# One named table load per normalising stage on ScalarE, in a kernel of a state-space block, attention and routed experts

## The reference

```python
# layer 0: normalise over 256 channels, split in 4 branches, scan each in 4 directions
xn = _ln(x, ln_g, ln_b)                      # xc * rsqrt(var + eps) * g + b
x = silu(conv3x3(xi @ in_W) + conv_b)        # each branch
delta = softplus(dts @ dt_W + dt_b)
h = h * exp(delta * A) + (delta * u) * B     # 2304 steps, 16 states; y = h . C
y = _ln(sum of the 4 directions, og, ob) @ out_W + skip_scale * xi
y = _ln(concatenate(outs), ln_g, ln_b) @ proj_W + proj_b
# layer 1: attention over all 4608 tokens, then 2 of 8 experts for each token
t = _ln_t(tokens)
f = t / max(norm(t), 1e-12)
a = softmax(f @ f.T) @ f
t1 = tokens + l2norm(0.8 * f + 0.2 * a)
out = t1 + sum over top 2 experts of p_e * (gelu(_ln_t(t1) @ W1_e + b1_e) @ W2_e + b2_e)
```

## Time and profile before

| | |
|---|---|
| runs of before | 6272.69, 6276.89, 6279.28 us (median 6276.89) |
| span of the profiled execution, first to last instruction | 6270.2 us |
| busy PE, DVE, ACT, POOL | 82%, 68%, 62%, 67% of the span |
| both norms, merge, project, blend | 0 to 98 us (with setup), 4085 to 4450, 4450 to 4613, 5536 to 5695 |
| scan | 780 to 4085 us |
| attention | 4613 to 5536 us |

### The profile page before, as it was taken

One profiled execution on the slowest core, in us unless ns is written; L12 is line 12 of the kernel. 1 busy time (PEld: TensorE's weight loads), 2 busy tenths in 40 slices (PEclk: granted clock), 3 DMA queues, 4 the chain that ended last, 5 costly groups with the idle time before them and its releaser, 6 DMA issues. The chain is left out here.

```text
span 6270.2 us, 83748 instructions
## 1 busy us (share of the span) xinstructions
PE 5167.0 (82%) x21564; PEld 3423.2 (55%) x21564; DVE 4275.8 (68%) x4244; ACT 3892.7 (62%) x8375; POOL 4196.6 (67%) x2703
## 2 busy tenths in 40 slices
PE   4666389999898898998989999845589999965997
PEld 2333155555555555555555555522358888844776
DVE  2666589999999999999999999956231111143433
ACT  2655488888888888888888888834532222233233
POOL 0566589999999999998999999933014444412343
PEclk8888599999999999999999999977789999975898
DMA  3454477777777777777777777764200000013213
GB/s 94 148 186 181 183 241 250 248 248 247 243 250 239 249 247 244 248 247 238 247 246 247 251 246 249 243 216 164 91 18 0 0 0 0 0 38 107 70 58 128
DMA packets 399686, 1073.56 MB, mean 171 GB/s; under 512 B 51470, under 2 KB 94511, under 8 KB 393600
## 3 DMA queue, kind: packets, MB, share of 16 engines
q1 hardware_dynamic: 384544, 1038.35, 49.7%
q0 software_dynamic: 7584, 20.72, 1.0%
q10 hardware_dynamic: 7104, 9.44, 0.5%
HBM read 883.39 MB, written 184.94 MB: 170 GB/s over the span
## 5 line engine op out<-in xcount | busy, mean ns | idle before, releaser
L918 POOL TENSOR_TENSOR scan_hc<-scan_h,scan_c_rep 128x768 f32<-128x768 f32 x1536 | 2749.4, 1824 | 236.7 <-PE scan_ps_y L749 171.4
L749 PE MATMUL scan_ps_y<-scan_hc,keep_ident 128*128 128x512 f32 (+1 forms) x6144 | 2217.2, 489 | 23.5 <-ACT scan_y L784 23.1
L883 DVE TENSOR_TENSOR_SCAN scan_h<-scan_da,scan_h,scan_ps_p 128x768 f32<-128x768 f32 x896 | 1567.8, 1794 | 0.0
L749 PEld LDWEIGHTS scan_ps_y<-scan_hc,keep_ident 128*128 128x128 f32 x6144 | 1066.6, 190 | 822.5 <-issue 737.6
L801 ACT ACTIVATE scan_warm<-scan_du_t 128x128 f32<-128x128 f32 x4608 | 1423.7, 388 | 40.7 <-PE scan_ps_p L740 35.3
L840 ACT ACTIVATE scan_da<-scan_dd,layer_a_neg 128x768 f32<-128x768 f32 x1344 | 1184.2, 921 | 2.2 <-issue 1.6
L1260 POOL TENSOR_TENSOR attn_e_lo<-attn_e,attn_e_hi 128x512 fp32r<-128x512 f32 x324 | 417.6, 1289 | 771.4 <-DVE attn_e_hi L1251 771.4
L740 PE MATMUL scan_ps_p<-keep_ident,scan_warm 128*128 128x128 f32 x4608 | 645.9, 277 | 221.9 <-DVE scan_h L883 221.1
L883 DVE TENSOR_TENSOR_SCAN scan_h<-scan_da,scan_ps_p 128x768 f32<-128x768 f32 x448 | 758.4, 1734 | 2.1 <-ACT scan_da L840 2.0
L740 PEld LDWEIGHTS scan_ps_p<-keep_ident,scan_warm 128*128 128x128 f32 x4608 | 531.5, 142 | 371.8 <-issue 160.4
L862 DVE TENSOR_TENSOR scan_ps_p<-scan_ps_p,scan_dd 128x768 f32<-128x768 f32 x576 | 546.6, 949 | 185.9 <-PE scan_ps_p L732 185.0
(11 more groups left out here) (291 smaller groups left out, 7109.4 us busy)
## 6 DMA issues: line engine op xcount, KB each, us to landing
scan_c_rep<-bc_dram SPq DMA_DIRECT2D x1536, 384.0 KB, 4.1
scan_dd<-dd_dram SPq DMA_DIRECT2D x96, 768.0 KB, 5.6
scan_b_rep<-bc_dram SPq DMA_DIRECT2D x192, 384.0 KB, 4.7
dd_dram<-delta_de SPq DMA_DIRECT2D x96, 384.0 KB, 6.5
dd_dram<-delta_du SPq DMA_DIRECT2D x96, 384.0 KB, 15.7
y_dram<-scan_y SPq DMA_DIRECT2D x96, 384.0 KB, 4.5
merge_y<-y_dram SPq DMA_DIRECT2D x32, 1152.0 KB, 10.3
delta_img<-xn_dram SPq DMA_DIRECT2D x16, 576.0 KB, 10.1
```

The source lines that it names most:

```text
L749: mm = pe.matmul(ps_y[:, lo:hi], keep["ident"][:, :], hc[t % HR][:, lo:hi], start=n == 0, stop=n == N - 1)
L883: dve.tensor_tensor_scan(view(h[n]), view(x), view(y), start, ALU.mult, ALU.add).then_inc(scan_done, 1)
L918: pool.tensor_tensor(hc[t % HR][:, :], h[t % N][:, :], c_rep[t % CR][:, :], ALU.mult).then_inc(hc_done, 1)
```

## The change

At the head of ScalarE's stream in four stage functions (five calls, as `norm_phase` is called twice) one call is added that loads a table set by name; the set holds Ln and Exp together.

```diff
@@ -46,6 +46,7 @@
 ROUND = 12582912.0
+LOG_EXP = "natural_log_exp_and_others"
@@ -253,6 +254,7 @@            (norm_phase)
         @block.scalar
         def _(act):
+            act.preload_act_table_set(LOG_EXP)
             with act.Fori(0, NTT // LN) as i:
```

## The result

The changed kernel takes 6235.96 us (median of 4 runs, 6227.41 to 6241.17) against 6277.69 for the kernel before on the same chip: ratio 0.9931, 95% interval 0.9912 to 0.9951. That is 42 us less, where 55 were forecast (6222 us, 6205 to 6237). A second measurement, on another chip, gave 6220.43 us (5 runs) against 6277.35: 0.9913, 0.9899 to 0.9927, which is 57 us less. The two intervals overlap; between them lies 0.992, about 50 us.

What follows compares the result with a forecast made beforehand. No engine is busy all the time; chains in the normalising stages make ScalarE's loads count where exposed. Loads 48.9, clashes 2.5 and clock 4 sum to 55.4 us, taken as 55: 6276.9 - 55 = 6222 us, range 6205 to 6237.

Steps and rivals of the forecast that it cites:

- The Exp's loads: All normalising stages: the table load ahead of each of 28 Exps is exposed, 1.43 us each, 40.0 us saved.
- the clock: TensorE in merge and project: shorter idle times may keep its granted clock from falling; 4 us gained, between -4 and 12.
- the clashes: Merge: VectorE and GpSimd taking turns on a shared port; shifted meeting dates bring +2.5 us net, between -8 and +12.
- The Ln's loads: Loads ahead of Ln, mostly hidden under TensorE's sums: 7.2 us saved in merge, 1.7 in project and blend, 0 in norms.
- The added loads: Five named loads ahead of ScalarE's first wait of each stage: hidden, cost 0; up to 5.1 us if four were uncovered.
- The page's 2.66 us a switch: Rival: every table load also stalls ScalarE for a drain, 2.66 us in all, giving 6186 us; chance 2%.
- the signs it named: In merge, if right: VectorE's L1019 mostly under 6 us, and L1003 longer than 2.88 us in most rounds.
- The norms: The two norm stages, four rounds: only the load ahead of Exp is exposed, 4 x 1.43 = 5.7 us saved.
- The total: Whole kernel: 48.9 + 2.5 + 4 = 55.4 us saved, forecast as 55, giving 6222 us.
- its own range: Whole kernel: 6209 to 6234 us, held at 71%, said to follow from the bounds of its uncertain terms.
- Merge gives its part back: Rival: GpSimd's turn in merge, bound to its input's landing, becomes the limit; 18.6 + 2.5 us missing, 6243 us; chance 10%.
- The built program has the same ones elsewhere: Setup, delta, scan and experts: no new table load appears there, as the built program keeps the same loads.

## Why the prediction was right, and which terms were mis-sized

- **The Exp's loads, 40.0 us:** the mechanism was right. 0.43 to 0.48 us from the last Ln's start to the first Exp in every round, and 44 us by the medians or 35 by the stages when they are put back. The sum taken alike in all stages was not: each is worth 1.8 us in project and blend, where the clock adds to it, and in merge, put back alone, nearly nothing, because of the clashes.
- **The Ln's loads, 8.9 us:** right. VectorE's wait in merge fell by 2.33 us, the sum of 0.90 and 1.43, and the Ln's loads put back cost 10.5 us by the medians and 5 by the stages, far from the 36 of full price.
- **The added loads, 0:** right, and three of the five are not needed at all.
- **The page's 2.66 us a switch:** by the rows 1.28 us; the Exp behind a put-back load starts 0.01 us after it. The Trainium skill (ScalarE: Activation LUTs, What ACT_TABLE_LOAD costs) has a drain in its sum that no run here shows as time of its own.
- **The clock, taken at 4 us, "nearer to 0, because both idle times are still long":** mis-sized. It is worth 1.1 us a round in merge (measured without the clash), some 9 us in eight rounds, and what project and blend gave over their loads, 15.7 + 14.9 - 24.6 = 6 us, is the same sign and is put down to it too (L1127 from 7.13 to 5.83 us). 15 us in place of 4. That the clock is what makes these steps long was tested by filling the idle time.
- **The clashes, taken at +2.5, between -8 and +12:** mis-sized, with the wrong sign. Without GpSimd's sum merge gains 26.8 us, with it 16.2: the clash takes back some 10 us. Merge scatters by 7 us between executions, so whether that is beyond the bound of -8 isn't certain. The prediction counted the two clashes as independent costs of each round. They are coupled: a late L1003 delays L1019 into GpSimd's next work, so both fall into one round and the next is free. Of the signs it named, L1019 is over 10 us in three rounds, as often as it was over 9 before, and L1003 is longer than 2.88 us in four rounds of eight, not in most.
- **The norms, 5.7 us:** 3.4 were found in the stage lengths. VectorE's wait for the Exp in norm1 fell from 9.23 to 7.81 us in each round, which is the forecast 1.42. TensorE's first step of a round there lies between 9.4 and 11.1 us in the traces of before and of the change, so norm1's rest of 1 us is within that scatter; norm0's of 1.5 us stays open.
- **The total:** the normalising stages give 50.2 us, and 42 and 57 us in the two measurements lie on both sides; delta and scan scatter by more than that difference. That 55 came so near is in part luck: the clock gave 11 us more than its term and the clashes took 13 more, and the two errors cancel. The first measurement, 6235.96 us, lies 1 us inside the range of 6205 to 6237, and outside what the prediction calls its own range, 6209 to 6234. That upper end doesn't follow from its terms either: clashes of -8 and a clock of -4 would give 6222 + 10.5 + 8 = 6240.
- **The rivals:** none came in. The nearest, "Merge gives its part back", had the mechanism (GpSimd's turn, bound to the landing of its input, becomes the limit), at some 10 us in place of its 21.
- **"The built program has the same ones elsewhere":** true, but I drew no rival from it. That a named load outlives its stage was to be seen in the built programs, and no rival had it.

## What to carry to other kernels

Price a removed instruction by its place, not by its length: between two steps of the same engine it shortens the chain by its length and a bit more, under the pace of the engine that feeds it by nothing. Whether the stage gets shorter by as much is a second question, and here merge and project answered it differently. When a chain gets shorter against a partner that keeps its own clock (here GpSimd, bound to a transfer), write down for two rounds in a row where they meet; one round alone misses the alternation. And before a table set is named in every stage, look how far one naming reaches.

## What the runs showed of the hardware

- The group of six VectorE steps with both inputs in SBUF (L1019 in the kernel before, L1021 in the changed one) takes 2.9 us alone and 10.6 us where GpSimd's sum runs beside it: the two engines take turns. The Trainium skill (SBUF — State Buffer, on the port pair that VectorE and GpSimd share) says that whichever starts first holds the pair for its whole instruction while the other waits, and the traces agree; the size, and that two such clashes can fall into one round and leave the next free, are this kernel's.
- Matmuls whose product nobody reads made the kernel faster. In project, 392 matmuls with 116.2 us of busy time in place of 240 with 95.6 came with a granted clock of 0.96 in place of 0.81, and the whole kernel stands at 0.9866 of before (0.985 to 0.9883) against 0.9913 for the change alone (0.9899 to 0.9927).
- A table load of 1.28 us put back ahead of every Exp cost 14.7 us in project (eight loads) and 0.6 us in merge (eight loads as well), against stage lengths of the change that differ by 2 us between its two traces.
